# Heads' sums turned in 32x32 squares on VectorE, and row maxima brought to rows by a transpose and two transfers through scratch DRAM

## Chip, cores and metric

The kernel runs on one core of a Trainium2 chip. The metric is the device time of one execution in microseconds; the time before is the median of three runs.

## What is computed

Eight sequences of 512 tokens with 256 features pass through four transformer layers with six attentions in all. Every attention has 16 heads of 16 features:

```python
q, k, v = x @ wq + bq, mem @ wk + bk, mem @ wv + bv      # split into 16 heads of 16
s = einsum('bhqd,bhkd->bhqk', q, k) * scale + bias        # window, causal or full
a = softmax(s)
o = einsum('bhqk,bhkd->bhqd', a, v).reshape(B, L, D)
out = o @ wo + bo                                         # then a residual and a layernorm
```

Attention 0 sees a window of 64 keys, attention 2 is causal, and 1, 3, 4 and 5 are full. After attentions 1, 3 and 4 comes a feed-forward block of 1024 hidden features. Everything is float32.

## The kernel before

A loop is one attention of one sequence. There are 48: the sequences go in pairs (slots), and within a pair the order is attention 0 of both, attention 1 of both and so on. All five engines run through one list of stages, PLAN, each taking its own part of every stage in order and waiting on semaphores for the others. The list for a loop is merged from four streams: 0 is the loop's own steps, 1 is the maxima of its later heads, 2 is the tail of the loop before (output product, feed-forward, layernorm) and the start of the next loop, and 3 is the context work of the next loop. The strings in MERGE say, digit by digit, from which stream the next stage comes; there is one string for each kind of loop.

**Scores and maxima.** The scores that go into the exponential come from bfloat16 parts that lie packed in rows of two tiles (q_packed and k_packed, line 686), with the query's negated row maximum as one more row, MAXROW. So the maximum has to be known, as a row over the queries, before a group's first scores. For that the scores are computed a second time, coarsely, queries on partitions (stage "max", line 655, 128 queries by up to 512 keys), and VectorE reduces them to one bfloat16 column of row_max for each head and block of 128 queries (line 921 where the attention is full, line 924 otherwise). Heads go in groups of four. When a group's 16 columns are there, stage "max_rows" follows: TensorE multiplies them by the identity (line 664, four matmuls of 128 columns into a score pair of PSUM), ScalarE copies the four rows to SBUF (line 817) and issues a transfer into MAXROW of q_packed (line 820). TensorE waits for it at the group's first scores (line 678).

**Steps.** A step is a group of heads and a block of 128 keys, 16 steps a loop. TensorE makes the scores of two heads at a time into one of two score pairs ("st"), ScalarE takes the exponential (line 834) and TensorE adds up the values of the four heads in four strips of 32 partitions of one bank ("pv", line 711); a 17th column of ones in the values gives the sums. After a group's last step ScalarE copies the bank to sums (line 843).

**Heads.** Stage "heads" turns sums, so that queries lie on partitions: four transposes on TensorE into one of the three banks "mx" (line 720), then VectorE's reciprocal of the 17th columns (line 933) and the multiply into tile o (line 935). At the end of the loop, in its tail, stage "turn_heads" turns o back, features on partitions, as the output product needs it: four transposes for each half of the features (line 727) into a score pair, copied to oT by ScalarE (line 847). The product (line 774, stage "rows", or line 748, stage "add") waits for these copies.

The three mx banks also take the maxima, the projections and the output products, and a bank is free again when VectorE (or ScalarE) has read it. Tile oT also holds "pre", the normalised input of attention 4. SyncE's queue carries the weights, the inputs and the bfloat16 parts through DRAM (lines 516 and 544); ScalarE's queue carries the maxima (line 820) alone. GpSimd masks the queries of a head for its maxima (line 1005), among other things.

Of the kernel before, what the change touches and what calls it, by code (L numbers as in the profile page):

```python
# [23 lines left out]
AHEAD = GRP + 2  # L24
RING = 4
# [88 lines left out]
def max_column(h, i):  # L114

    return ((NG - 1 - h // GRP) * TT + i) * GRP + h % GRP


def maxima_stages(b, a, heads):

    for h in heads:
        if h and h + RING - 1 < H:
            yield "mask", b, a, h + RING - 1
        for i in range(TT):
            yield "max", b, a, h, i
        if h % GRP == GRP - 1:
            yield "max_rows", b, a, h // GRP

# [54 lines left out]
def prefetched(b, a):  # L183

    return a == 0 and b >= SLOTS
# [45 lines left out]
def streams(j):  # L231
# [14 lines left out]
    "first": "022001141101110111001111444141110101111000111101101141110410111010111011011001141012222222222202"  # L246
           "422444242444224244424244444220204042200242222402200422240220044000400",
    "01": "011101122111011201111212112301210111301101111011012011110211002121012001100111210110012122222322"
           "22020220200222020220020222022000222202220200222",
    "10": "010013001101113022110120111101021212222020101100110112111010110100011211010110101121101011001021"  # L250
           "131222222222020222002020222020022202000220022220200220202202000",
    "11": "011011022111012110212122220201010221110101121100101111211121220001210111000112222220020112011021"
           "10110210001010012222220222220202022202202022202220220020022222022020002202000",
    "20": "011110101121210121111101211222220022111021011100101110211002222001211101221212220102010101101110"
           "0012011000220021222222222222020222022220002022220222000222220222022200",
    "21": "030011212111013010110011111210111011211011011100101102111221222113111211021101010101210012020022"
           "2222022020222020202202202202202000200222202022020220002",
    "30": "010110221110121102121122222321103011011011100110201101112101100001111100010110101101101011001010"
           "213222222222020222002020222020022202000220022220200220202202000",
    "31": "011011022111012110212122220201010221123310333233111211112111123311132111102222202021123201102200"  # L260
           "022210202001120010110201112100021222223322202202202022002202022202002202000002222200022020220200"
           "0",
    "40": "011011022111012110212122220201010221123310333233111211112111123311132111102222202021123220110220"
           "002220202001120002111001121101002122222332220220220202200220202220200220200000222220002202022020"
           "00",
    "41": "011011020111032231100102111211011121112111121111211311112011021101200110010110100110031000012222"
           "22222002220220202202020222002020200222202022000220200200000000",
    "50": "011011020111032231100102111211011121112111121111211311112011022211012001100101101001100310000122"
           "2222222002220220202202020222002020200222202022000220200200000000",
# [883 lines left out]
```

## Time and profile before

| | |
|---|---|
| median of three runs | 3678.9 us (3677.79 to 3679.34) |
| profiled execution | 3676.84 us |
| its span | 3675.0 us |
| mean granted TensorE clock | 0.996 |
| instructions | 56922 |

The span reaches from the first to the last instruction of the program in the profile; the 1.8 us between it and the execution's time lie around it. The profile counts an engine as busy while one of its instructions runs; matmuls are pipelined and overlap in it.

### The profile page before, as it was taken

The numbers are of one execution on the slowest core, as the hardware profiler recorded it, in microseconds if no ns is written. First come the engines' busy times: TensorE is split into PE (matmuls) and PEld (weight loads), VectorE is DVE, ScalarE is ACT, GpSimd is POOL, SyncE is SP. The second block draws the span as 40 slices with busy tenths as digits, with TensorE's granted clock in tenths as the row PEclk, the third lists the DMA queues.
The fourth block names the chain that finished last, engine by engine and source line by source line (L and its number), as shares of the span: only waits on it lengthen the run. The fifth ranks groups of instructions, "written<-read, shape, count | busy, mean of one in ns | idle before, by whom it ended". The sixth has DMA issues, their size and how long they took to land.

```text
span 3675.0 us, 56922 instructions
## 1 busy us (share of the span) xinstructions
PE 3594.9 (98%) x20572; PEld 1822.7 (50%) x20852; DVE 2355.5 (64%) x6039; ACT 2083.7 (57%) x2663; POOL 1140.6 (31%) x1053
## 2 busy tenths in 40 slices
PE   8999999999999999999999999999999999999998
PEld 5555545443554555544364555554436455455443
DVE  4765776655675586665677558665567855766556
ACT  2555565555555565655656546555575655655555
POOL 4322432222532242222253223222235322322222
PEclk9999999999999999999999999999999999999999
DMA  6312311212321231121232122112133212211111
GB/s 222 104 44 75 104 53 52 84 58 87 106 74 47 75 104 44 52 84 58 87 122 84 47 85 69 47 63 71 63 108 106 85 52 84 71 42 62 61 52 52
DMA packets 260119, 279.28 MB, mean 76 GB/s; under 512 B 25074, under 2 KB 251250, under 8 KB 255858
## 3 DMA queue, kind: packets, MB, share of 16 engines
q1 hardware_dynamic: 258308, 274.84, 22.9%
q8 instruction: 170, 2.79, 0.3%
q14 instruction: 105, 0.86, 0.1%
q10 hardware_dynamic: 1536, 0.79, 0.1%
HBM read 195.05 MB, written 79.69 MB: 75 GB/s over the span
## 4 chain that ended last, share of the span: by engine, by line
PE 92%; DVE 3%; ACT 2%; issue 2%; SPq 1%; DMA 0%; ACTq 0%; POOL 0%; DVEq 0%; POOLq 0%; another core or an unknown queue 0%
PE pv L711 16%; PE st L686 15%; PE mx L655 14%; PE mx L774 10%; PE mx L630 9%; PE st L738 9%; PE st L639 5%; PE mx L748 4%; PE mx L720 2%; PE mx L771 2%; ACT probs L834 2%; PE st L664 1%; PE st L784 1%; DVE mx L924 1%; PE st L727 1%
## 5 line engine op out<-in xcount | busy, mean ns | idle before, releaser
L834 ACT ACTIVATE probs<-st 128x1024 f32<-128x1024 f32 (+1 forms) x1344 | 1261.1, 977 | 643.4 <-PE st L686 401.1
L921 DVE TENSOR_REDUCE row_max<-mx 128x1 bf16<-128x512 f32 x2048 | 1293.9, 687 | 421.9 <-PE mx L655 271.3
L1005 POOL TENSOR_TENSOR qm<-q_high,own_rows 128x512 bf16<-128x512 bf16 x768 | 791.7, 1039 | 1643.6 <-PE mx L655 1033.1
L686 PE MATMUL st<-q_packed,k_packed 97*128 97x512 bf16 (+2 forms) x3072 | 810.5, 344 | 24.7 <-issue 9.2
L655 PE MATMUL mx<-k_high,qm 128*128 128x512 bf16 (+4 forms) x2792 | 797.2, 341 | 14.0 <-DVE row_max L924 2.8
L711 PE MATMUL pv<-probs,va 128*32 128x512 f32 (+2 forms) x6144 | 703.4, 531 | 8.9 <-ACT probs L834 6.9
L655 PEld LDWEIGHTS mx<-k_high,qm 128*128 128x128 bf16 x3072 | 281.9, 97 | 485.3 <-issue 116.2
L686 PEld LDWEIGHTS st<-q_packed,k_packed 97*128 97x128 bf16 (+1 forms) x3072 | 279.6, 98 | 402.9 <-ACT probs L834 122.9
L924 DVE CUSTOM_DVE_ANT_0 mx<-mx,tab 128x192 f32<-128x192 f32 (+4 forms) x1024 | 402.5, 443 | 108.1 <-PE mx L655 103.1
L738 PE MATMUL st<-xT,w1s 128*128 128x512 f32 x768 | 343.3, 593 | 1.9 <-ACT xT L863 1.5
L948 DVE TENSOR_TENSOR y<-mx,row 128x256 f32<-128x256 f32 x224 | 95.0, 424 | 345.1 <-PE mx L774 340.7
L1017 POOL TENSOR_TENSOR rstd<-spread_of,m_half 128x2 f32<-128x2 f32 x144 | 99.3, 690 | 691.8 <-DVE spread_of L967 691.8
L854 ACT ACTIVATE hid<-st,col 128x512 f32<-128x512 f32 x192 | 121.4, 683 | 253.7 <-PE st L738 253.7
L711 PEld LDWEIGHTS pv<-probs,va 128*32 128x32 f32 x6144 | 124.9, 108 | 251.3 <-issue 178.4
L774 PE MATMUL mx<-w2s,hid 128*128 128x256 f32 x1024 | 231.6, 380 | 0.0
L738 PEld LDWEIGHTS st<-xT,w1s 128*128 128x128 f32 x768 | 144.8, 190 | 157.4 <-issue 149.0
L774 PEld LDWEIGHTS mx<-w2s,hid 128*128 128x128 f32 x1024 | 190.0, 191 | 22.7
L630 PE MATMUL mx<-xT,sq 128*128 128x512 f32 x352 | 165.2, 615 | 9.3 <-DMA sq<-squares_dram 8.0
L774 PE MATMUL mx<-sq,oT 128*128 128x256 f32 x640 | 164.7, 380 | 0.0
L863 ACT ACTIVATE xT<-st,col 128x256 f32<-128x256 f32 x192 | 96.7, 561 | 106.1 <-PE st L784 106.1
L817 ACT ACTIVATE max_rows<-st 4x512 bf16<-4x512 f32 x192 | 111.2, 579 | 72.0 <-PE st L664 71.4
L843 ACT ACTIVATE sums<-pv 128x512 f32<-128x512 f32 x192 | 114.8, 598 | 62.4 <-PE pv L711 58.8
(93 smaller groups left out, 3525.3 us busy)
## 6 DMA issues: line engine op xcount, KB each, us to landing
k_packed<-k_parts_dram SPq DMA_DIRECT2D x576, 128.0 KB, 2.7
q_packed<-q_parts_dram SPq DMA_DIRECT2D x576, 128.0 KB, 2.7
q_parts_dram<-q_low SPq DMA_DIRECT2D x96, 256.0 KB, 2.1
k_parts_dram<-k_low SPq DMA_DIRECT2D x96, 256.0 KB, 2.1
q_parts_dram<-q_high SPq DMA_DIRECT2D x48, 256.0 KB, 2.1
k_parts_dram<-k_high SPq DMA_DIRECT2D x48, 256.0 KB, 2.2
w1s<-w_dram SPq DMA_DIRECT2D x12, 1024.0 KB, 5.0
w2s<-w_dram SPq DMA_DIRECT2D x12, 1024.0 KB, 7.2
```

The lines of the kernel that those rows point to most:

```text
L630: mm = pe.matmul(bank, sqw(f"{m}{a}")[:, j, t * P:(t + 1) * P], src[:, j, :], start=(j == 0), stop=(j == KT - 1))
L639: mm = pe.matmul(pair[:, i // 2, i % 2 * D:(i % 2 + 1) * D], source(b, a)[:, j, i * P:(i + 1) * P], sqw(f"v{a}")[:, j, :], start=(j == 0), ...
L655: mm = pe.matmul(bank[:, 0:k1 - k0], qm[:, h % RING, i * P:(i + 1) * P], high["k"][s][:, t, k0:k1], start=True, stop=True)
L686: mm = pe.matmul(flat[:, c:c + w], kk[:, k * P:(k + 1) * P], qq[:, q0:q1], start=True, stop=(k_kind == FULL))
L711: mm = pe.matmul(pv[j * PAIR:(j + 1) * PAIR, q0:q1], va[s][:, k, at:at + PAIR], probs[:, step % 2, c:c + q1 - q0], start=(k == 0 and k_kin ...
L738: mm = pe.matmul(pair[:, e], w1s[:, j, at:at + P], xT[s][:, j, :], start=(j == 0), stop=(j == KT - 1))
L748: mm = pe.matmul(bank, weight[:, j, t * P:(t + 1) * P], src[:, j, :], start=(j == 0), stop=(j == count - 1))
L774: mm = pe.matmul(bank[:, 0:D], src[:, j, i * P:(i + 1) * P], weight[:, j, :], start=False, stop=(j == count - 1))
L834: act.activation(dst[:, :, 0:w], held["scores", b, a, n, e][:, :, 0:w], ACT.Exp, scale=ATT_SCALE[a]) \
L921: ins = dve.tensor_reduce(top, scores, AX_X, ALU.max, negate=True)
L924: ins = dve.tensor_tensor_reduce(scores, scores, hide[:, hide.shape[1] - (k1 - k0):hide.shape[1]], -1.0, 1e30, ALU.add, ALU.min, top)
L1005: pool.tensor_tensor(qm[:, h % RING], high["q"][s][:, h // HT], own_rows[:, h % HT:h % HT + 1].to_broadcast([P, TOK]), ALU.mult) \
```

## The change

Stage "heads" leaves TensorE. VectorE transposes sums in SBUF in squares of 32x32 (tile turned), takes the reciprocal, multiplies into a second tile (normal), and after every second group transposes that tile in squares straight into oT. A strip of 32 partitions holds one head's 17 rows, so a square holds one head and 32 queries; two groups fill the 32 rows of a strip with 16 + 16 features, which puts the heads in another order, place(h). The columns of the value weights, their biases and the rows of the output weights are put in that order on the host. Stage "turn_heads", with its matmuls and its copies on ScalarE, is gone; the output product waits for VectorE. "pre" moves from oT to the first part of the tile hid.

Stage "max_rows" leaves TensorE too. VectorE transposes the group's block of row_max (128 partitions by 32 columns, bfloat16) in squares, ScalarE issues a transfer to scratch DRAM that puts the pieces in order (128 pieces of 64 bytes), and in a new stage "max_back", placed behind the maxima of the next group's first head (for the last group, directly behind max_rows), ScalarE waits for this transfer and issues another, 4 KB, into MAXROW of q_packed. All MERGE strings are new.

```diff
+def place(h):
+    return h // HT * HT + h % GRP * 2 + h // GRP % 2
...
 def max_column(h, i):
-    return ((NG - 1 - h // GRP) * TT + i) * GRP + h % GRP
+    return h // GRP * BLK + h % GRP * TT + i
...
             yield "max_rows", b, a, h // GRP
+        if h % GRP == 0 and h or h == H - 1:
+            yield "max_back", b, a, (h - 1) // GRP
...
     yield "heads", b, a, NG - 1
-    yield "turn_heads", b, a, 0
-    yield "turn_heads", b, a, 1
...
-            return {"ctx": ncT, "pre": oT}.get(tag, xT[b % SLOTS])
+            return {"ctx": ncT, "pre": pre}.get(tag, xT[b % SLOTS])
...
-                elif kind == "max_rows":
-                    a, g = stage[2:]
-                    pe.wait_ge(*mx_drained.past(("max", b, a, g * GRP + GRP - 1, TT - 1)))
-                    pair = held["row", b, a, g] = st_pair()
-                    for i in range(TT):
-                        c = max_column(g * GRP, i)
-                        mm = pe.matmul(pair[:, 0, i * P:(i + 1) * P], row_max[s][:, c:c + P], tb("eye"), start=True, stop=True)
-                    mm.then_inc(*st_filled.mark(("row", b, a, g)))
...
-                elif kind == "heads":
-                    a, g = stage[2:]
-                    pe.wait_ge(*sums_kept.past(("sums", b, a, g)))
-                    bank = held["heads", b, a, g] = mx_bank()
-                    for i in range(TT):
-                        mm = pe.transpose(bank[:, i * P:(i + 1) * P], sums[:, g % 2, i * P:(i + 1) * P], eye[:])
-                    mm.then_inc(*mx_filled.mark(("heads", b, a, g)))
-                elif kind == "turn_heads":
...
                 elif kind == "max_rows":
                     a, g = stage[2:]
-                    act.wait_ge(*st_filled.past(("row", b, a, g)))
-                    act.activation(max_rows[:, g % 2], held["row", b, a, g][0:GRP, 0], ACT.Identity) \
-                        .then_inc(*st_drained.mark(("row", b, a, g)))
-                    act.wait_ge(*st_drained.past(("row", b, a, g)))
-                    act.dma_start(packed["q"][MAXROW:MAXROW + 1, g * GRP:(g + 1) * GRP], max_rows[:, g % 2]) \
+                    act.wait_ge(*row_step.past(("max_rows", b, a, g)))
+                    act.dma_start(r_dram[g].rearrange("(r k) c -> k r c", k=P // BLK), max_rows[:, g]).then_inc(max_row_out[g], 16)
+                elif kind == "max_back":
+                    a, g = stage[2:]
+                    act.wait_ge(max_row_out[g], 16 * (LOOP_NO[b, a] + 1))
+                    act.dma_start(packed["q"][MAXROW:MAXROW + 1, g * GRP:(g + 1) * GRP], r_dram[g, 0:GRP * TT * P // BLK]) \
                         .then_inc(max_row_in[g], 16)
...
-                        act.wait_ge(*mx_filled.past(("heads", pb, pa, (g - 2) % NG)))
+                        act.wait_ge(*row_step.past(("turned", pb, pa, (g - 2) % NG)))
...
+                elif kind == "max_rows":
+                    a, g = stage[2:]
+                    j = LOOP_NO[b, a]
+                    if j:
+                        dve.wait_ge(max_row_out[g], 16 * j)
+                    dve.wait_ge(*mx_drained.past(("max", b, a, g * GRP + GRP - 1, TT - 1)))
+                    dve.transpose(max_rows[:, g], row_max[s][:, g * BLK:(g + 1) * BLK]) \
+                        .then_inc(*row_step.mark(("max_rows", b, a, g)))
                 elif kind == "heads":
                     a, g = stage[2:]
-                    dve.wait_ge(*mx_filled.past(("heads", b, a, g)))
...
+                    t, odd = divmod(g, 2)
+                    old = (b, a, g - 1) if g else (*before(b, a), NG - 1) if LOOP_NO[b, a] else None
+                    blocks = turned[:].rearrange("p (n c) -> p n c", c=BLK)
+                    shares = normal[:].rearrange("p (n c) -> p n c", c=BLK)[:, :, odd * HD:(odd + 1) * HD]
+                    dve.wait_ge(*sums_kept.past(("sums", b, a, g)))
+                    if old:
+                        dve.wait_ge(*row_step.past(("shares", *old)))
+                    chain(dve.transpose(turned[:], sums[:, g % 2]), ("turned", b, a, g))
+                    chain(dve.reciprocal(rec[:], blocks[:, :, HD]), ("rec", b, a, g))
+                    if old and not odd:
+                        dve.wait_ge(*row_step.past(("oT", old[0], old[1], old[2] // 2)))
+                    share = dve.tensor_tensor(shares, blocks[:, :, 0:HD],
+                                              rec[:].unsqueeze(2).to_broadcast([P, TOK // BLK, HD]), ALU.mult)
+                    share.then_inc(*row_step.mark(("shares", b, a, g)))
+                    if odd:
+                        if LOOP_NO[b, a] and not t:
+                            pb, pa = before(b, a)
+                            dve.wait_ge(*mx_filled.past(("add", pb, "a4", KT - 1) if pa == 4 else ("rows", pb, f"a{pa}", TT - 1)))
+                        dve.wait_ge(*row_step.past(("shares", b, a, g)))
+                        dve.transpose(oT[:, t], normal[:]).then_inc(*row_step.mark(("oT", b, a, t)))
...
+    for a in range(6):
+        square[f"v{a}"], square[f"o{a}"] = square[f"v{a}"][:, order], square[f"o{a}"][order]
...
+        args.append(nc.dram_tensor("rows_of_max_dram", (NG, P, BLK), BF16, kind="Internal").ap())
```

## Rows read from the trace of the kernel before

**Rows 1.** The page: span, engines' busy time, the chain's shares by line.
```profile
span 3675.0 us, 56922 instructions
...
PE 3594.9 (98%) x20572; PEld 1822.7 (50%) x20852; DVE 2355.5 (64%) x6039; ACT 2083.7 (57%) x2663; POOL 1140.6 (31%) x1053
...
PE pv L711 16%; PE st L686 15%; PE mx L655 14%; PE mx L774 10%; PE mx L630 9%; PE st L738 9%; PE st L639 5%; PE mx L748 4%; PE mx L720 2%; PE mx L771 2%; ACT probs L834 2%; PE st L664 1%; PE st L784 1%; DVE mx L924 1%; PE st L727 1%
```

**Rows 2.** Timeline of TensorE, two windows: start us, busy us, engine, line, count.
```profile
100.31 0.63 PE L720 MATMUL mx<-eye,sums 128*128 128x128 f32 x4
100.77 0.60 PE L727 MATMUL st<-eye,o 128*128 128x128 f32 x4
101.21 0.30 PE L655 MATMUL mx<-k_high,qm 128*128 128x128 bf16 x2
...
2598.15 0.40 PE L664 MATMUL st<-tab,row_max 128*128 128x128 bf16 x4
2598.39 0.60 PE L655 MATMUL mx<-k_high,qm 128*128 128x512 bf16 x2
2598.82 0.60 PE L686 MATMUL st<-q_packed,k_packed 97*128 97x512 bf16 x2
2599.25 0.38 PE L655 MATMUL mx<-k_high,qm 128*128 128x512 bf16 x1
...
2600.21 1.07 PE L711 MATMUL pv<-probs,va 128*32 128x512 f32 x8
```

**Rows 3.** Groups by line: count | busy us, mean ns | idle us before.
```profile
L720 PE MATMUL mx<-eye,sums 128*128 128x128 f32 x768 | 116.5, 274 | 0.8 <-ACT sums L843 0.7
...
L817 ACT ACTIVATE max_rows<-st 4x512 bf16<-4x512 f32 x192 | 111.2, 579 | 72.0 <-PE st L664 71.4
...
L935 DVE TENSOR_TENSOR o<-mx,rec 128x256 f32<-128x256 f32 x192 | 81.5, 425 | 6.6
...
L664 PE MATMUL st<-tab,row_max 128*128 128x128 bf16 x768 | 75.2, 221 | 2.4 <-DVE row_max L924 2.4
...
L727 PE MATMUL st<-eye,o 128*128 128x128 f32 x384 | 58.4, 279 | 0.6 <-DVE o L935 0.4
L847 ACT ACTIVATE oT<-st 128x512 f32<-128x512 f32 x96 | 56.2, 595 | 7.2 <-PE st L727 7.2
...
L933 DVE RECIPROCAL rec<-mx 128x16 f32<-128x16 f32 x192 | 48.2, 251 | 13.6 <-PE mx L720 13.0
```

**Rows 4.** VectorE by line; for L921 and L973 duration ns min/median/max.
```profile
L962 DVE BATCH_NORM_STATS2 st<-y 128x6 f32<-128x256 f32 x288 | 107.9, 417 | 2.1
...
L967 DVE TENSOR_SCALAR spread_of<-moments 128x2 f32<-128x2 f32 x144 | 24.4, 169 | 5.0
...
L921 DVE TENSOR_REDUCE row_max<-mx x2048: 680/684/697, 132.8 to 3637.6; 128x1 bf16<-128x512 f32 x187
...
L973 DVE TENSOR_SCALAR y<-y,moments,rstd x288: 401/408/1426, 117.5 to 3667.6; 128x256 f32<-128x256 f32 x144
```

**Rows 5.** Windows, one loop each: length; busy us (count) PE, PEld, DVE, ACT, POOL; PEclk.
```profile
1051.70:1117.60 65.90, 64.97 (x358) 28.48 (x366) 52.34 (x99) 43.90 (x53) 23.02 (x21) 1.00 0.24 75
1859.40:1905.20 45.80, 44.60 (x431) 30.14 (x428) 35.50 (x167) 24.02 (x35) 30.23 (x27) 1.00 0.36 114
1616.90:1708.00 91.10, 89.84 (x395) 37.10 (x400) 48.40 (x81) 48.97 (x59) 20.76 (x18) 1.00 0.19 60
```

**Rows 6.** DMA issues: count, KB, us to landing; for L820 the issue's ns.
```profile
k_packed<-k_parts_dram SPq DMA_DIRECT2D x576, 128.0 KB, 2.7
...
q_parts_dram<-q_low SPq DMA_DIRECT2D x96, 256.0 KB, 2.1
...
L820 ACTq DMA_DIRECT2D q_packed<-max_rows x192: 580/581/1174, 27.6 to 3640.5; - x192
```

**Rows 7.** Timeline at the start of a loop, and the window from there on.
```profile
1002.37 0.26 PE L686 MATMUL st<-q_packed,k_packed 106*128 106x192 bf16 x1 [2.45 <-DMA q_packed<-q_parts_dram]
...
1002.40:1005.80 3.40, 3.40 (x28) 3.26 (x29) 1.96 (x10) 1.41 (x2) 3.28 (x4) 0.70 0.31 109
```

More of the change, by code:

```diff
@@ L276 @@
+    "last": "011100111101000021111100101211110112112100100011011101112111010100110110011001100101101001120000"
+           "020102020200000002000000",
 }
@@ L347, in program @@
         va = [sb(f"va{s}", [P, TT, VROW]) for s in range(SLOTS)]
-        row_max = [sb(f"row_max{s}", [P, TT * H + P], BF16) for s in range(SLOTS)]
+        row_max = [sb(f"row_max{s}", [P, NG * BLK], BF16) for s in range(SLOTS)]
         ncT = sb("ncT", [P, KT, TOK])
         oT = sb("oT", [P, KT, TOK])
-        o = sb("o", [P, TT, D])
+        turned = sb("turned", [P, TOK])
+        normal = sb("normal", [P, TOK])
         y = sb("y", [P, TT, D])
@@ L358, in program @@
         qm = sb("qm", [P, RING, TOK], BF16)
-        max_rows = sb("max_rows", [GRP, 2, TOK], BF16)
+        max_rows = sb("max_rows", [P, NG, BLK], BF16)
         probs = sb("probs", [P, 2, GRP * TOK])
@@ L363, in program @@
         x_next = [hid[:, s * KT:(s + 1) * KT] for s in range(SLOTS)]
+        pre = hid[:, 0:KT]
         flat_hid, flat_w1, flat_w2 = (t[:].rearrange("p k n -> p (k n)") for t in (hid, w1s, w2s))
@@ L426, in program @@
         packed_in = [sem(f"packed{half}_in") for half in range(2)]
+        max_row_out = [sem(f"max_row{g}_out") for g in range(NG)]
         max_row_in = [sem(f"max_row{g}_in") for g in range(NG)]
@@ L624, in _ @@
                         pe.wait_ge(sq_in[a], 16)
-                    src = (oT if a == 4 else x_next[s] if prefetched(b, a) else xT[s]) if m == "q" else source(b, a)
+                    src = (pre if a == 4 else x_next[s] if prefetched(b, a) else xT[s]) if m == "q" else source(b, a)
                     pe.wait_ge(*(input_of(b, a) if m == "q" else keys_of(b, a)))
@@ L714, in _ @@
                     mm.then_inc(*step_done.mark(("values", b, a, n)))
-                elif kind == "heads":
-                    a, g = stage[2:]
-                    pe.wait_ge(*sums_kept.past(("sums", b, a, g)))
-                    bank = held["heads", b, a, g] = mx_bank()
-                    for i in range(TT):
-                        mm = pe.transpose(bank[:, i * P:(i + 1) * P], sums[:, g % 2, i * P:(i + 1) * P], eye[:])
-                    mm.then_inc(*mx_filled.mark(("heads", b, a, g)))
-                elif kind == "turn_heads":
-                    a, t = stage[2:]
-                    pe.wait_ge(*mx_drained.past(("heads", b, a, (t + 1) * NG // KT - 1)))
-                    pair = held["oT", b, a, t] = st_pair()
-                    for i in range(TT):
-                        mm = pe.transpose(pair[:, 0, i * P:(i + 1) * P], o[:, i, t * P:(t + 1) * P], eye[:])
-                    mm.then_inc(*st_filled.mark(("oT", b, a, t)))
                 elif kind == "hidden":
@@ L1050 @@
     zeros = np.zeros(D, np.float32)
+    order = np.zeros(D, int)
+    for h in range(H):
+        order[place(h) * HD:(place(h) + 1) * HD] = np.arange(h * HD, (h + 1) * HD)
     kv2 = L2("Wkv")
@@ L1064 @@
     inner = {f"{m}{a}": L1(f"{pre}_{m}_W") for a, pre in ((2, "sa"), (3, "ca")) for m in "qkv"}
+    for a in range(6):
+        square[f"v{a}"], square[f"o{a}"] = square[f"v{a}"][:, order], square[f"o{a}"][order]
+    for a in FOLDED:
+        outer[f"v{a}"] = outer[f"v{a}"][:, order]
     vec = {}
@@ L1076 @@
         vec[f"b{m}4"] = zeros
+    for a in range(6):
+        vec[f"bv{a}"] = vec[f"bv{a}"][order]
     vec["bo4"] = L2("bo")
```

83 lines of the change are left out of this document (35 added, 48 removed).

## Prediction

> **What bounds the kernel now.** I read the page first: TensorE is busy for 3594.9 of 3675.0 us, VectorE for 64%, ScalarE for 57% [rows 1]. A busy matmul record overlaps its neighbour, so the shares by line of the chain that ended last say more; its first ten lines are all TensorE's, and "mx L720" (turning the heads' sums) holds 2% of the span, "st L664" (maxima to rows) 1% and "st L727" (turning the heads) 1%. The timeline then gives what one such group takes from the engine, from its start to the start of the next one [rows 2]: four L720 transposes 0.46 us (100.31 to 100.77), four L727 transposes 0.44 us (to 101.21), four L664 matmuls 0.24 us (2598.15 to 2598.39). Two maxima of a full loop take 0.43 us, two scores 0.43 us, a step's values 1.07 us. So TensorE is a queue with few holes, and what matters is work taken off it and holes put into it.
>
> **The change part by part.** The profiled execution took 3676.8 us (span 3675.0 and 1.8 us around it), 2.1 us under the median of 3678.9; I sum changes and add them to the median.
>
> *A. Matmuls that go.* By count and pitch: four matmuls to a group, 192 groups of L720 x 0.46 = 88 us, 192 of L664 x 0.24 = 46 us, 96 of L727 x 0.44 = 42 us [rows 2, 3]. Together -176 us. The chain's shares of 2, 1 and 1% of 3675 (147 us as rounded) agree in size.
>
> *B. Holes and buffers that go with them.* TensorE idled 0.8 + 2.4 + 0.6 = 3.8 us right before these groups [rows 3]. ScalarE's copies L817 (111.2 us) and L847 (56.2 us) go, so 288 fewer jobs hold one of the two score pairs in PSUM and 192 fewer hold a max bank. ScalarE is 2% of the chain, 74 us, which is the most that this can give. I take -8, nearer to the 3.8 us seen; bounds 0 and -74.
>
> *C. VectorE's new work.* The trace has no square transpose. Nearest are operations from SBUF: 417 ns for 256 elements (L962) and 169 ns for 2 (L967), a slope of 0.98 ns an element, so 0.67 us for 512 elements and 0.2 us for the 32 of a max block; from PSUM, 512 elements take 684 ns (L921) [rows 4]. Bounds for 512: 0.42 us (as for 256) and 2.7 us (four times L921, if a 4-byte element went byte by byte). I take 0.68, since one pass over the elements is what the rows show for every kind of operation. Reciprocal and multiply stay. A loop (there are 48) gets four turns of sums, two of heads and four small ones: 6 x 0.68 + 4 x 0.2 = 4.9 us, in all 235 us, and VectorE goes from 64% to about 72%. In a loop like 1616.9 to 1708.0 it idles for 43 us and this is hidden by TensorE's own work [rows 5]. 24 loops are tight (VectorE at 0.69 or more of the window): 16 like 1051.7 to 1117.6 (52.3 of 65.9 us busy) and 8 like 1859.4 to 1905.2 (35.5 of 45.8). After a saving of 3.5 us the first kind has 57.2 of 62.4 us, the second 40.4 of 42.3. In-order waits don't let an engine reach 95%; at 92% the second kind needs 43.9 us, 1.6 more, x 8 = 13 us, and I give the first 0.75 us each, 12 us. So +25; bounds 0 and all new work of the tight loops, 24 x 4.9 = 118. Behind a turn on VectorE stand the row maxima that free the three max banks: an odd group now holds the engine for 0.68 + 0.25 + 0.42 + 0.68 = 2.0 us, where it was 0.7.
>
> *C2. A port.* One VectorE operation wholly in SBUF (L973) took 1426 ns where 408 is its median [rows 4]; the difference, 1018 ns, is about one GpSimd mask operation (23.02 us for 21 in [rows 5], 1.1 each). A few such hits among 192 multiplies that now read SBUF twice would be some us of VectorE's time, mostly under cover; I add nothing. The Trainium skill (SBUF — State Buffer, "SBUF: two separate sides") has a rule that speaks against the change: a VectorE operation with two SBUF inputs and a GpSimd operation lock a port pair against each other, and the loser waits for the whole instruction. The trace agrees with a lock of that length; by the rule with every multiply hit the sum would be up to 192 x 1.0 us of VectorE time worse, which is what the rival "VectorE bounds" covers.
>
> *D. The rows come later.* Before, one 4 KB transfer from SBUF. Now VectorE turns a block, ScalarE issues a write to scratch DRAM, and at the stage "max_back" waits for it and issues the read. Nearest landings: 2.1 us for a write to scratch DRAM, 2.7 us for a read [rows 6]. Walking the new stage list with the pitches above, 20 of the 192 reads stand less than 2.7 us of TensorE's work ahead of the scores that need them: loops of attention 4 at groups 2 and 3 (0.4 and 1.3 us, four times each), of attention 3 at group 0 (1.5, four times), attention 0 (1.7, three times), the very last group (0.0), and four more. The shortfalls add to 26 us. TensorE waits there with nothing behind it, in order. +26; bounds 0 (TensorE is itself late) and 46 (each wait 1.0 us longer, if the clock falls as it did after the 2.45 us hole at 1002.37: there it was 0.70 on the mean of 3.4 us, a mix of 1.2 and 2.4 GHz, which costs 0.30 x 3.4 = 1.0 us [rows 7]).
>
> *E. ScalarE's waits.* Its issue takes 0.58 us [rows 6]; a copy of 0.58 goes for each issue that comes, and L847 goes besides, so its work falls by 56 us. But it now stands at "max_rows" for VectorE's last max and turn (159 of 192 such stages stand 0.4 us or less of TensorE's work behind the last max), and at "max_back" for the landing: in 32 groups less than 2.1 us of TensorE's work lies between, short by 34 us in sum. Queued behind are the exponentials; TensorE feels it once both score pairs are full. With ScalarE 57% busy I let half of the 34 through, 17, and 8 for the stands at max_rows: +25; bounds 0 and 100.
>
> *F. The sums' path to the output product.* TensorE's and ScalarE's parts are gone, VectorE's chain is 2.0 us. Four times (second half, attention 1) only 0.8 us of TensorE's work lies between: +5; bounds 0 and 15. "pre" moves to another tile and the weights' columns are reordered on the host: 0. The second read-out of oT waits for the previous product, which stands far ahead in all but four loops, and there just ahead: 0.
>
> Sum: -176 - 8 + 25 + 26 + 25 + 5 = -103, so 3678.9 - 103 = 3576 us. A measurement of this kernel tells 0.2% (7.4 us) from no change.
>
> **The rivals.**
> *Nearly all of it hides* (3505 to 3545, -176 - 8 and then 10 to 50 of the costs). For: 24 loops with idle VectorE; the shortfalls of D fall where TensorE may be late anyway. Against: 20 reads with too little ahead. Chance 0.17.
> *VectorE or ScalarE's queue bounds the short loops* (3615 to 3670). C at 80, D at 40, E at 60 give -176 - 8 + 80 + 40 + 60 + 5 = +1, the far end; with half of each excess over the forecast's terms, 52 us, it is 3628. For: 95% in eight loops, locks. Against: TensorE was 99% busy at 79% VectorE. Chance 0.15.
> *Squares are slow, and the kernel slower.* Place: the turns in the 24 tight loops. Price: these have 65.9 - 3.5 - 52.3 = 10.1 us to spare, less 0.8 for the small turns, so 1.55 us for each of six; above it a loop grows by six times the excess. The gain of 103, with the 25 of C, is used up at 1.55 + 128 / (24 x 6) = 2.44 us a turn; the bound of 2.7 us gives 24 x 6 x 1.15 = 166 us in place of the 25, +38 net, 3717 (3690 to 3850, the other loops having too little cover at its upper end). For: no row shows the operation. Against: every VectorE row is one pass. Chance 0.10.
> *The matmuls go but the time does not*: their time turns into waits on the same VectorE work, within 7.4 us of before. It needs A eaten exactly. Chance 0.04.
>
> **How the numbers follow.** The forecast itself, 3545 to 3615, has 0.52; its two neighbours, both faster, 0.17 and 0.15; under 3505 us 0.02; slower 0.10; same 0.04. The range of 8 in 10 is 3512 to 3668: it holds the forecast and nearly all of its two neighbours, and leaves out the slower case. Faster is the sum of the first four, 0.86; same 0.04, slower 0.10.
>
> **What would show it.** L664, L720 and L727 are gone, the span is about 100 us shorter, and TensorE's idle time grows by some 50 to 80 us. A 128x512 transpose takes 0.6 to 0.75 us (over 1.5: the slow rival). VectorE's share is 71 to 74%. In the list of waits, scores wait for a transfer q_packed<-scratch some 20 times, at attention 4 most of all (else D is wrong); ScalarE's exponentials wait, and TensorE for them, more often than before (E). The tight loops shorten by about 2 us and the others by 3 to 3.5 us (C). A kernel that is slower, or 170 us faster, would prove the size of C to E wrong.

## The result and the profile after

The changed kernel took 3581.1 us (median of four runs, 3578.2 to 3585.4), where the kernel before took 3678.4 beside it: ratio 0.9737, 95% interval 0.9720 to 0.9754, 97 us faster. The forecast was 3576 us (3512 to 3668).

The head of the page, and the chain of waits by engine and by line:

```profile
span 3579.2 us, 53643 instructions
...
PE 3472.6 (97%) x18932; PEld 1656.1 (46%) x18932; DVE 2579.5 (72%) x6519; ACT 1933.9 (54%) x2375; POOL 1145.7 (32%) x1053
...
PE 83%; DVE 12%; ACT 1%; issue 1%; DMA 1%; SPq 1%; POOL 1%; ACTq 0%; DVEq 0%; POOLq 0%
PE pv L712 15%; PE st L687 14%; PE mx L664 13%; PE mx L762 10%; PE st L725 9%; PE mx L639 9%; DVE row_max L905 5%; PE mx L736 4%; PE st L648 4%; DVE mx L908 3%; PE mx L759 2%; PE st L772 1%; DVE y L976 1%; DMA rows_of_max_dram<-max_rows 1%; DVE turned L928 1%
```

Against [rows 1]: TensorE's busy time fell by 122.3 us and its idle time rose from 80.1 to 106.6 us, by 26.5 where the prediction had said 50 to 80. (The trace before lacks 280 of TensorE's matmul records, 20572 beside 20852 weight loads, so both of its figures are a little off.) The three groups that were to leave the chain have left it; VectorE now holds 12% of it, mostly with row maxima. The groups on VectorE (count | busy us, mean ns | idle us before):

```profile
L905 DVE TENSOR_REDUCE row_max<-mx 128x1 bf16<-128x512 f32 x2048 | 1283.4, 684 | 230.9 <-PE mx L664 226.6
L928 DVE STREAM_TRANSPOSE turned<-sums 128x512 f32<-128x512 f32 x192 | 134.6, 701 | 5.4 <-ACT sums L832 5.4
L932 DVE TENSOR_TENSOR normal<-turned,rec 128x256 f32<-128x256 f32 x192 | 90.6, 472 | 6.6
L940 DVE STREAM_TRANSPOSE oT<-normal 128x512 f32<-128x512 f32 x96 | 68.3, 711 | 6.6
L929 DVE RECIPROCAL rec<-turned 128x16 f32<-128x16 f32 x192 | 48.7, 254 | 6.6
L917 DVE STREAM_TRANSPOSE max_rows<-row_max 128x32 bf16<-128x32 bf16 x192 | 40.6, 212 | 20.7 <-DVE row_max L905 0.9
```

The turns take 0.70, 0.71 and 0.21 us, 243.5 us in all (forecast 0.68, 0.68, 0.2 and 235). The list of waits (engine, line, waited for: us, times, longest):

```profile
PEld mx L664 <- DVE row_max L905: 193.0, 338, 1.3
PEld st L687 <- ACT probs L823: 148.9, 228, 0.8
PEld mx L664 <- DVE row_max L908: 83.3, 227, 0.9
PE mx L664 <- DVE row_max L905: 18.2, 54, 1.0
PE mx L664 <- DVE row_max L908: 12.9, 38, 0.7
ACT probs L823 <- DMA rows_of_max_dram<-max_rows: 12.0, 2, 9.2
ACT q_low L792 <- DMA rows_of_max_dram<-max_rows: 11.0, 11, 2.2
...
PEld st L687 <- DMA q_packed<-rows_of_max_dram: 1.5, 1, 1.5
...
PE st L687 <- DMA q_packed<-rows_of_max_dram: 0.6, 1, 0.6
```

The maxima's weight loads wait 276 us for VectorE, where it was 153 (103.8 and 49.5). The scores' wait for the maximum's row, of which the forecast had 20, happens once, in the last group of all. ScalarE's queue (duration ns: min/median/max):

```profile
L805 ACTq DMA_DIRECT2D rows_of_max_dram<-max_rows x192: 510/526/1096, 25.6 to 3543.9; - x192
L809 ACTq DMA_DIRECT2D q_packed<-rows_of_max_dram x192: 200/200/252, 33.3 to 3546.5; - x192
```

Three windows of the changed kernel (us, then busy us by engine, clock, DMA share): the first loop kind and the second, both tight before, and a roomy one.

```profile
1028.80:1092.40 63.60, 62.41 (x323) 24.74 (x323) 56.86 (x109) 40.77 (x47) 22.23 (x21) 1.00 0.25 79
1811.30:1854.70 43.40, 41.87 (x392) 26.78 (x390) 36.58 (x167) 20.39 (x29) 28.15 (x26) 1.00 0.39 123
1480.00:1578.80 98.80, 96.42 (x466) 47.69 (x466) 71.32 (x160) 53.87 (x70) 26.14 (x27) 1.00 0.21 69
```

The first two answer to [rows 5]: the loop of 66.0 us is 63.6 with VectorE at 0.89, the one of 45.8 is 43.4 at 0.84. The third is the surprise: it was 99.0 us, ten groups of matmuls are gone from it (3.7 us by pitch: 4 x 0.46, 4 x 0.24, 2 x 0.44), VectorE idles 28% of it, and it is 0.2 us shorter. Cut at each loop's last copy of sums, and leaving out the first loop, the tight loops give 1.8 us each on the mean, the roomy ones 2.4. These means hide a wide spread. Of the tight ones, attention 3 of the first sequence gives 5.3 us (65.6 to 60.3, VectorE 0.78 busy before), which is more than the 3.7 us of matmuls that it lost, and attention 0 of the second sequence gets longer. Of the roomy ones, attention 4 (second sequence) and 5 (first sequence) give 4.4 and others 0.3.

### The profile page after: what moved, and what is told of

The parts are those of the page before. It is cut to its first block, busy times and chain, and to the rows that moved or that the text cites. A ratio compares the mean times of both kernels' runs of the same rounds, so it can differ in the third digit from the quotient of the medians.

```text
span 3579.2 us, 53643 instructions
## 1 busy us (share of the span) xinstructions
PE 3472.6 (97%) x18932; PEld 1656.1 (46%) x18932; DVE 2579.5 (72%) x6519; ACT 1933.9 (54%) x2375; POOL 1145.7 (32%) x1053
## 4 chain that ended last, share of the span: by engine, by line
PE 83%; DVE 12%; ACT 1%; issue 1%; DMA 1%; SPq 1%; POOL 1%; ACTq 0%; DVEq 0%; POOLq 0%
PE pv L712 15%; PE st L687 14%; PE mx L664 13%; PE mx L762 10%; PE st L725 9%; PE mx L639 9%; DVE row_max L905 5%; PE mx L736 4%; PE st L648 4%; DVE mx L908 3%; PE mx L759 2%; PE st L772 1%; DVE y L976 1%; DMA rows_of_max_dram<-max_rows 1%; DVE turned L928 1%
## 5 line engine op out<-in xcount | busy, mean ns | idle before, releaser
L664 PE MATMUL mx<-k_high,qm 128*128 128x512 bf16 (+4 forms) x3072 | 883.2, 345 | 41.8 <-DVE row_max L905 18.2
L664 PEld LDWEIGHTS mx<-k_high,qm 128*128 128x128 bf16 x3072 | 282.2, 97 | 609.2 <-DVE row_max L905 193.0
L687 PEld LDWEIGHTS st<-q_packed,k_packed 97*128 97x128 bf16 (+1 forms) x3072 | 280.3, 98 | 439.7 <-ACT probs L823 148.9
L639 PE MATMUL mx<-xT,sq 128*128 128x512 f32 x352 | 163.7, 611 | 10.5 <-DMA sq<-squares_dram 8.0
L908 DVE DVE_READ_ACCUMULATOR2_ANT row_max<- 128x1 bf16 x1024 | 147.2, 144 | 0.0
```

Source lines behind the costliest of these rows:

```text
L639: mm = pe.matmul(bank, sqw(f"{m}{a}")[:, j, t * P:(t + 1) * P], src[:, j, :], start=(j == 0), stop=(j == KT - 1))
L664: mm = pe.matmul(bank[:, 0:k1 - k0], qm[:, h % RING, i * P:(i + 1) * P], high["k"][s][:, t, k0:k1], start=True, stop=True)
L687: mm = pe.matmul(flat[:, c:c + w], kk[:, k * P:(k + 1) * P], qq[:, q0:q1], start=True, stop=(k_kind == FULL))
L908: ins = dve.tensor_tensor_reduce(scores, scores, hide[:, hide.shape[1] - (k1 - k0):hide.shape[1]], -1.0, 1e30, ALU.add, ALU.min, top)
```

## Experiments

All of them are against a kernel before of 3677 to 3679 us on the same chip. The changed kernel's own run is 3581.1; it was not run again beside them, so a difference to it compares two chips, on which the kernel before agrees within 1 us. The edits shown are the main lines of each, "..." where lines are left out.

### What the matmuls were worth

**doubled**: the kernel before, with each matmul of L664, L720 and L727 issued twice.

```diff
-                    for i in range(TT):
+                    for i in [*range(TT)] * 2:
```

> The kernel before, with every matmul of lines 664, 720 and 727 issued twice into the same place; nothing else. The forecast's term A (176 us for them once, by their pitch on TensorE): 3678 + 176 = 3854 us, 3835 to 3870. Rival: part of these matmuls lies in waits that were there anyway, and what the change gained, 97 us, is all that they cost: 3775 us, 3755 to 3795.

3818.0 us, ratio 1.0379 (1.0361 to 1.0396): +140, where the pitches say 176, and between the two expectations. TensorE's busy time rose by 170 us (to 3765.3) and its idle time fell from 80.1 to 50.6. So part of such a matmul fits where TensorE waited anyway. If removing is worth what adding costs, which this run doesn't show, the change takes away about 0.8 of the pitch.

**turn_twice**: the same test on the changed kernel, with the four transposes of stage "turn" (L772) twice, 56 us by pitch.

```diff
-                    for j in range(KT):
+                    for j in [*range(KT)] * 2:
```

> The changed kernel with the four TensorE transposes of each stage "turn" issued twice, some 56 us of TensorE's work by pitch. Doubling VectorE's turns cost 120 us for 134 us of work. Theory 1 (the changed kernel sits where both engines set the pace by turns): 35 to 55 us slower than the changed kernel, as TensorE's doubled work in the kernel before cost 0.8 of its pitch. Rival (VectorE alone now sets the pace): less than 15 us slower.

3626.3 us (0.9860 of before, 0.9846 to 0.9875): +45, again 0.8. TensorE still sets the pace after the change, at the same price.

### What VectorE's turns cost

**short_turns**: the changed kernel, with the two large turns cut to 32 of 512 columns from the second loop on (it leaves work out: the rest of turned and oT keeps the first loop's values, so its output is not the kernel's).

```diff
+                    w = BLK if LOOP_NO[b, a] else TOK
-                    chain(dve.transpose(turned[:], sums[:, g % 2]), ("turned", b, a, g))
+                    chain(dve.transpose(turned[:, 0:w], sums[:, g % 2, 0:w]), ("turned", b, a, g))
...
-                        dve.transpose(oT[:, t], normal[:]).then_inc(*row_step.mark(("oT", b, a, t)))
+                        dve.transpose(oT[:, t, 0:w], normal[:, 0:w]).then_inc(*row_step.mark(("oT", b, a, t)))
```

> The changed kernel, but from the second loop on the turns of sums and of heads on VectorE cover 32 of the 512 columns (work left out: the rest of both tiles stays as the first loop left it). That takes some 0.5 us off each of 282 turns, 140 us of VectorE's time. Theory 1, the forecast's split (all new VectorE work costs 25 us of the path): 25 x 140/224 = 16 us faster than the changed kernel, 3560 to 3572. Theory 2, from the trace after (the maxima wait for banks that VectorE frees late, and this is most of what was given back, some 70 us): 40 to 60 us faster, 3520 to 3541.

3565.4 us (0.9692, 0.9677 to 0.9706): -16, though VectorE's busy time fell by 113.5 us (2579.5 to 2466.0).

**two_turns**: the changed kernel, with sums turned twice.

```diff
+                    chain(dve.transpose(turned[:], sums[:, g % 2]), ("first", b, a, g))
```

> The changed kernel with the turn of sums on VectorE done twice, one after the other: 192 x 0.70 = 134 us more of VectorE's time. Theory 1: the 24 tight loops are close to full now, so half of their 67 us come out, the other 24 hide theirs: 20 to 40 us slower than the changed kernel, 3601 to 3621. Theory 2: VectorE already sets the pace in the tight loops and bursts stall TensorE elsewhere: 60 to 110 us slower, 3641 to 3691.

3700.7 us (1.0061, 1.0046 to 1.0076): +120, all of the gain, and more than either expectation. Busy time, and the chain by engine:

```profile
PE 3501.4 (95%) x18932; PEld 1656.8 (45%) x18932; DVE 2737.8 (74%) x6711; ACT 1937.1 (52%) x2375; POOL 1144.7 (31%) x1053
...
PE 64%; DVE 29%; issue 3%; ACT 2%; DMA 1%; SPq 1%; POOL 1%; ACTq 0%; DVEq 0%; POOLq 0%
```

And the group of its multiply:

```profile
L933 DVE TENSOR_TENSOR normal<-turned,rec 128x256 f32<-128x256 f32 x192 | 118.0, 615 | 6.8 <-DVE rec L930 0.2
```

VectorE's busy time rose by 158 us, not 135: the multiply behind the turns now takes 615 ns on the mean (below). Going down by 113 us of VectorE's work gave 16, going up by 158 cost 120, so on this engine removing and adding are not worth the same. The changed kernel stands at the bend, and VectorE's share, 72 or 74%, doesn't show where the bend is.

### The way of the rows through scratch DRAM

**one_hop**: the rows go from SBUF to MAXROW directly, in four pieces, with no scratch DRAM and no "max_back".

```diff
-                    act.dma_start(r_dram[g].rearrange("(r k) c -> k r c", k=P // BLK), max_rows[:, g]).then_inc(max_row_out[g], 16)
+                    for k in range(P // BLK):
+                        act.dma_start(packed["q"][MAXROW:MAXROW + 1, g * GRP:(g + 1) * GRP]
+                                      .rearrange("p h (i k c) -> p (h i) k c", k=P // BLK, c=BLK)[:, :, k],
+                                      max_rows[k * BLK:k * BLK + GRP * TT, g]).then_inc(max_row_in[g], 16)
```

> The changed kernel without the scratch DRAM: ScalarE sends the turned maxima straight into the row in four pieces of 16 partitions each; the stage max_back and its wait are gone. ScalarE issues four transfers a group instead of two, 192 x 2 x 0.58 = 223 us more of its time. Theory 1 (terms D and E: late rows and ScalarE's waits cost 51 us): faster by 20 to 40 us, 3541 to 3561, the added issues taking the rest. Theory 2 (late rows cost nothing, ScalarE's waits little): the added issues decide, 0 to 50 us slower, 3581 to 3631.

3738.8 us (1.0164, 1.0149 to 1.0180): +158, where the dearer expectation had +50 at most. The one landing takes 1.7 us (median), but what counts is the queue (the chain by engine; then the issues, ns min/median/max):

```profile
PE 68%; DVE 13%; ACTq 7%; ACT 6%; issue 3%; POOL 1%; SPq 1%; DMA 1%; DVEq 0%; POOLq 0%
```

```profile
L806 ACTq DMA_DIRECT2D q_packed<-max_rows x768: 510/611/1572, 26.1 to 3700.1; - x192
```

768 issues at 0.61 us are about 470 us of ScalarE's sequencer, where the changed kernel has 192 x (0.53 + 0.20) = 140. The exponentials stand behind them: TensorE's scores wait 55.8 us for them and their loads 233.9 (148.9 in the changed kernel). This kernel has a dearer queue besides having one hop, so it doesn't price the scratch hop by itself.

**pool_back**: "max_back", wait and issue, goes to GpSimd's queue.

```diff
-                    act.wait_ge(max_row_out[g], 16 * (LOOP_NO[b, a] + 1))
-                    act.dma_start(packed["q"][MAXROW:MAXROW + 1, g * GRP:(g + 1) * GRP], r_dram[g, 0:GRP * TT * P // BLK]) \
+                    pool.wait_ge(max_row_out[g], 16 * (LOOP_NO[b, a] + 1))
+                    nc.gpsimd.dma_start(packed["q"][MAXROW:MAXROW + 1, g * GRP:(g + 1) * GRP], r_dram[g, 0:GRP * TT * P // BLK]) \
```

> The changed kernel, but GpSimd instead of ScalarE waits for the write to scratch DRAM and issues the read, at the same place in the order. It takes the wait and 0.2 us of issue a group off ScalarE. Theory 1 (term E: ScalarE's waits cost 17 us): 10 to 20 us faster than the changed kernel, 3561 to 3571. Theory 2 (ScalarE has slack, the trace after shows 23 us of such waits in all): within 7 us, 3574 to 3588. Rival: GpSimd's masks come late behind its wait, slower by over 10 us.

3731.9 us (1.0141, 1.0124 to 1.0158): +151. GpSimd, idle two thirds of the time, waits in order:

```profile
POOL q_packed L1009 <- DMA rows_of_max_dram<-max_rows: 812.6, 154, 23.5
...
PEld mx L664 <- POOL qm L1003: 62.5, 46, 4.1
...
PE mx L664 <- POOL qm L1003: 40.5, 29, 3.6
```

Queued behind its wait are the masked queries, and TensorE waits for those: 62.5 us by the loads, where it was 14.4 in the changed kernel, and 40.5 by the matmuls, where it was 0.7. That is not all of the 151. VectorE's busy time is 68.5 us longer too (2648.0; the multiply takes 657 ns on the mean), TensorE's own waits for row maxima are 76.4 us (31.1), and its mean clock is 0.981 (0.993). How the loss splits among these was not tested. A wait costs what stands behind it.

**late_back**: the changed kernel with "max_back" moved later in the list where less than 2.6 us of TensorE's work lay between it and the write, if 3.3 us stayed ahead of the scores.

```diff
+        while done < 12 and ahead - WORK.get(stages[at][0], 0) >= 15:
+            done, ahead = done + WORK.get(stages[at][0], 0), ahead - WORK.get(stages[at][0], 0)
+            at += 1
+        stages.insert(at, back)
```

> The changed kernel, with the stage that waits for the write and issues the read moved later wherever less than 2.6 us of TensorE's work lies between it and the write, as long as 3.3 us are left ahead of the scores. Theory 1 (ScalarE's waits for the landing, 24 us by the list of waits, reach TensorE by a third or less): 3 to 10 us faster than the changed kernel. Rival (they are hidden by ScalarE's idle time): within 3 us. Rival (reads then come late for scores, as the forecast's step D had it): slower by 10 us or more, with scores waiting for q_packed<-rows_of_max_dram more than once.

3577.9 us (0.9729, 0.9712 to 0.9745): 3 us less, not to be told from none. ScalarE's waits for the write don't get fewer (30.5 us in sum, 23.6 in the changed kernel) and only stand elsewhere:

```profile
ACT probs L844 <- DMA rows_of_max_dram<-max_rows: 18.0, 5, 7.5
...
ACT q_high L808 <- DMA rows_of_max_dram<-max_rows: 12.5, 1, 12.5
```

One of 12.5 us is in the first loop, whose DMA share is 0.68 (in the changed kernel). So moving these waits gains nothing that can be measured.

### Instructions and order, apart

The change has new instructions and a new order (the MERGE strings). The next five kernels part them. "Old rows" are TensorE's matmul and ScalarE's copy; "old heads" are L720 and L727 on TensorE. In the new order the old instructions had no stages of their own, so I had to place them: rows at "max_back", turn_heads three and five stages behind the last "heads".

**rows_back**: new order and heads, old rows.

```diff
+                elif kind == "max_back":
+                        mm = pe.matmul(pair[:, 0, i * P:(i + 1) * P], row_max[s][:, c:c + P], tb("eye"), start=True, stop=True)
...
+                    act.activation(max_rows[:, g % 2], held["row", b, a, g][0:GRP, 0], ACT.Identity) \
```

> The changed kernel with the maxima's rows made as before (four matmuls, ScalarE's copy, one transfer from SBUF), all at the place of the stage max_back in the new order; heads stay on VectorE. TensorE gets 44 us more by pitch, 35 us by the rate of the doubled matmuls (140 for 176). Theory X, both parts gain by their matmuls' share (97 x 44/169 = 25 us): 3606 us, 3598 to 3615. Theory Y, the two transfers and ScalarE's waits (what short turns did not give back, some 27 us) eat the gain of this part: 3575 to 3592 us.

3678.5 us (0.9995, 0.9986 to 1.0005): +97, where the expectations had 34 at most. TensorE's busy time is only 28 us longer (3500.7); the other 71 us are idle time (177.6), spread over many waits: 14.2 us of the row matmuls for the exponentials that hold the score pairs, 10.5 of the scores for the transfer, and smaller ones.

**heads_back**: new order and rows, old heads.

```diff
+        if stage[0] == "heads" and stage[3] == NG - 1:
+            due = [(3, ("turn_heads", *stage[1:3], 0)), (5, ("turn_heads", *stage[1:3], 1))]
...
+                        mm = pe.transpose(bank[:, i * P:(i + 1) * P], sums[:, g % 2, i * P:(i + 1) * P], eye[:])
```

> The changed kernel with the heads' sums turned on TensorE as before, and the turn of heads after the last group three and five stages later, or just ahead of the product; the maxima's rows stay on VectorE and scratch DRAM. Theory X: 72 us slower than the changed kernel, 3653 us, 3640 to 3665. Theory Y (the heads' part brought the whole gain of 97): 3670 to 3685. Should VectorE's turns be worth little, as short turns says (16 us for 140), TensorE's 125 us by pitch x 0.8 = 100 us less that 24 us: 3657 us.

3800.4 us (1.0332, 1.0316 to 1.0347): +219, where the expectations ended at 3685 us. TensorE's busy time is 121 us longer, its idle time 98. Part of that idle time comes from where I placed turn_heads, since the output product waits for its copies (0.7 us in the kernel before):

```profile
PE mx L787 <- ACT oT L864: 18.1, 25, 1.1
```

**both_back**: both edits, so that only the order is new.

> The changed kernel with both parts undone, so the old instructions in the new order of stages. Theory 1: the order is worth little by itself, 3668 to 3690 us, so the gain is that of the two parts. Rival: the new order alone brings part of the gain, 3630 to 3665. Other rival: it is made for the new instructions, and old ones in it stall, over 3700.

3890.8 us (1.0577, 1.0561 to 1.0593): 212 us slower than before. The waits for the copies of oT (18.1 us) and for the rows' transfer (10.5) are here too, so the 212 are not the order's alone.

**new_in_old_order**: the other corner. The old strings, with "max_back" by the change's rule, but for the last group up to four stages behind max_rows; both turns into oT at the last group, where the old order has room for them.

```diff
+            n = at["max", b, a, (g + 1) * GRP, TT - 1] if g + 1 < NG else \
+                min(at["max_rows", b, a, g] + 4, at["scores", b, a, g * TT, 0] - 1)
+            behind.setdefault(n, []).append(("max_back", b, a, g))
...
-                    if odd:
+                    if g == NG - 1:
```

> The new instructions in the order of the kernel before. Its opposite, the old instructions in the new order, took 3890.8 us, 212 more than before. Theory 1 (each order fits its own instructions: the new one leaves VectorE its time where it has turns to make): the old order costs the new instructions 60 us or more, 3640 or longer, with TensorE's waits on VectorE's row maxima longer than 193.0 + 83.3 us. Theory 2 (the order only names the stages differently; the gain is that of the instructions): within 15 us of the changed kernel's 3581. Theory 3 (the old order suits everything that keeps VectorE late): between 3595 and 3640, so the gain is part instructions, part order.

3866.7 us (1.0516, 1.0500 to 1.0531): 189 us slower than before with the same number and kinds of instructions that are 97 us faster in the new order. The turns into oT stand elsewhere than in the changed kernel, though, and that counts below. Its waits:

```profile
PEld mx L678 <- DVE row_max L919: 270.1, 375, 3.3
...
PE mx L678 <- DVE row_max L919: 116.3, 118, 2.9
...
PE mx L678 <- DVE row_max L922: 72.1, 76, 3.3
```

TensorE's own waits for maxima are 188.4 us, where the changed kernel has 31.1. How one comes about, first on VectorE, then on TensorE (start us, busy us, group; idle before in brackets):

```profile
1607.46 0.68 DVE L919 TENSOR_REDUCE row_max<-mx 128x1 bf16<-128x512 f32 x1
1608.06 0.70 DVE L942 STREAM_TRANSPOSE turned<-sums 128x512 f32<-128x512 f32 x1
1608.80 0.25 DVE L943 RECIPROCAL rec<-turned 128x16 f32<-128x16 f32 x1
1609.08 0.42 DVE L946 TENSOR_TENSOR normal<-turned,rec 128x256 f32<-128x256 f32 x1
1609.61 1.30 DVE L957 STREAM_TRANSPOSE oT<-normal 128x512 f32<-128x512 f32 x2
1610.84 3.05 DVE L919 TENSOR_REDUCE row_max<-mx 128x1 bf16<-128x512 f32 x5
```

```profile
1608.35 0.38 PE L678 MATMUL mx<-k_high,qm 128*128 128x512 bf16 x1
1611.55 1.21 PE L678 MATMUL mx<-k_high,qm 128*128 128x512 bf16 x2 [2.83 <-DVE row_max L919]
```

From 1608.06 on VectorE turns for 2.8 us while TensorE is due to make maxima. The three mx banks are full, so TensorE stands for 2.83 us, and it stands in order: nothing behind the maximum starts either. Behind it the clock falls too: its mean is 0.969 in this kernel and 0.993 in the changed one, and with the same 18932 instructions TensorE is busy 3571.7 instead of 3472.6 us. Against the changed kernel, the profiled span is 286 us longer, 99 of it busy time and 187 idle time. Summing TensorE's idle time in the 5 us from the start of each of the 192 turns of sums gives 207.8 us here and 32.8 in the changed kernel. By groups of a loop it is 26.5, 29.4, 31.6 and 120.4 us here and 3.6, 2.2, 21.5 and 5.6 there. So more than half stands behind the last group, as in the burst shown, where two turns into oT follow each other because I placed them so; the old strings with one turn a group were not built. The rest, 87.5 against 27.3 us, has no such burst and points at the order. In the window of this loop VectorE is busy for 66%, so it had the time; it was asked at the wrong moment.

**rows_only**: the kernel before and its order, with only the rows new.

> The kernel before with only the maxima's rows made in the new way (VectorE's small transpose, write to and read from scratch DRAM, each stage where the old order puts it); the heads stay on TensorE. It takes away 192 groups of L664, 46 us by pitch and 37 at the 0.8 that doubling showed, and 111 us of ScalarE's copies, and adds 192 x 0.21 = 41 us to VectorE. Theory 1 (the transfers' waits are covered): 20 to 40 us faster than before, 3638 to 3658. Rival (ScalarE's stands at the write and at the read cost as much as the copies did): within 10 us of before. Rival (the old order has too little room for the landings): slower than before by over 15 us, with scores or exponentials waiting for the scratch transfers by over 60 us.

3693.1 us (1.0045, 1.0030 to 1.0060): 16 us slower than before; my range had been 20 to 40 faster. Of the waits:

```profile
ACT q_low L820 <- DMA rows_of_max_dram<-max_rows: 50.4, 17, 3.3
...
ACT L871 <- DMA rows_of_max_dram<-max_rows: 27.9, 8, 3.8
...
ACT sums L860 <- DMA rows_of_max_dram<-max_rows: 14.3, 3, 11.3
ACT q_high L815 <- DMA rows_of_max_dram<-max_rows: 12.0, 1, 12.0
...
PEld st L701 <- DMA q_packed<-rows_of_max_dram: 6.4, 4, 2.8
PE st L701 <- DMA q_packed<-rows_of_max_dram: 5.4, 5, 1.9
```

ScalarE waits 109 us for the writes (the four rows shown and 4.0 more), against 23.6 in the changed kernel: in the old order "max_back" comes too soon behind the write. By loops, most are 0.6 to 1.1 us shorter; the first is 12 longer, the others of attention 0 together 13, and eight of attentions 3 and 4 together 16.

| rows / heads | old order | new order |
|---|---|---|
| old / old | 3678 (before) | 3891 |
| new / old | 3693 | 3800 |
| old / new | not built | 3678 |
| new / new | 3867 | 3581 (the change) |

(Old rows with new heads in the old order would need a second oT: there the heads of group 1 stand up to 58 stages ahead of the product that still reads the first.) The old instructions lose 212 us by the new order and the new ones gain 286, both with the placement of the stages that I chose for them. The rows alone, in the old order, are worth nothing (16 us slower); the heads alone were not built there, but added to the rows they make the old order 174 us slower. Undoing one part in the new order costs 97 or 219, more than the whole change gave, so such a number is not that part's own worth.

## Why the prediction was right, and where it was not

- **The total** held: -97 for -103. If removing the matmuls gave what doubling them cost, two errors of 36 and 30 us cancelled in it (A and the rest, below), and that was luck.
- **A (the matmuls, -176)** was over-priced, as far as doubling tells. The doubling measured 140. The step that failed was "by count and pitch": a pitch is what a group occupies once it is reached, not what the end moves by; the engine had waits that the group could fill. The 147 us of the chain's shares, which I read as agreement in size, lies near 140 by rounding: unrounded the three shares are 74.9, 50.5 and 36.7 us, 162 in all.
- **B (-8)** was not tested apart. ScalarE's copies went, its busy share fell from 57 to 54%.
- **C (VectorE, +25).** The turn was sized right (0.70 for 0.68), so the rival "squares are slow" fell at once. The cost is of the right size: taking away 113.5 of the 243.5 us was worth 16 us. The tight loops shortened by 1.8 us, forecast 2, but that is a mean of -4.7 to +5.3, so its fit is luck. The roomy ones gave 2.4 and not 3 to 3.5, as unevenly. The split into tight and roomy loops by VectorE's share, and the limit of 92% on an engine that waits in order, had no row behind them: in [rows 5] TensorE, which waits in order too, is busy for 98.6% of a loop, and the two kinds of tight loops ended with VectorE at 0.89 and 0.84. The runs fit another reading better: what counts is what VectorE does when TensorE wants a bank. two_turns shows how close the rival "VectorE bounds" was: 135 us more of such work costs 120.
- **C2 (the port, nothing added)** was small here (9 us of VectorE's time) but real: see below.
- **D (late rows, +26)** was wrong. The walk counted TensorE's work by pitch and took it that TensorE arrives on time; one of the 20 waits was seen, in the place with 0.0 us of room, and the reads land in time elsewhere.
- **E (ScalarE's waits, +25)** was too high. The read's issue takes 0.20 us and not 0.58, and ScalarE waits 23.6 us for writes where I let 34 in and passed on half. At max_rows it waits 34.9 us for VectorE's small turn, of which 8 were passed on. Moving the waits for the writes (late_back) changed nothing that can be measured; what the others cost was not tested.
- **F (+5)**: the product waits 4.7 us for oT in all, 3.0 of that at the end of the kernel; fits.
- **Together**, B to F were forecast at +73 and came to 140 - 97 = 43, a remainder that hangs on the 140. Of these, short_turns accounts for 16, and the loops of attention 0 (second sequence) and the first loop, which became 7.9 and 3.4 us longer in sum, for 11. There (the third such loop) TensorE stands for 3.7 us for q_packed<-q_parts_dram (2.0 before), and the clock falls behind it:

```profile
1855.00:1858.70 3.70, 0.03 (x1) 0.00 (x0) 0.60 (x4) 0.00 (x0) 0.20 (x1) 0.91 0.61 180
1858.70:1862.40 3.70, 3.68 (x21) 3.35 (x22) 1.15 (x7) 1.38 (x2) 1.04 (x1) 0.50 0.64 192
1862.40:1869.20 6.80, 6.80 (x23) 3.77 (x22) 4.08 (x10) 1.61 (x3) 0.00 (x0) 0.82 0.44 137
```

(window, busy us of PE, PEld, DVE, ACT and POOL, granted clock, DMA share.) After a hole of 3.7 us TensorE runs 3.7 us at 0.50, the 1.2 GHz level. Why these parts come later in the new order, I did not test. The last 16 us are unassigned.

What the forecast left out is the order. It priced the new list as it stood, which was enough for the total, but called the gain that of the instructions. The runs show that these instructions are 189 us slower than before in the old list, with the turns into oT placed as said.

## What to carry to other kernels

Work moved to an engine with idle time needs its place in the order as much as its time: ask which buffers fill while the in-order engine does it, and merge the stages anew before judging the move, since one part tried alone in the old order can look useless. Doubling what is to be removed gives a price before it is removed (here 0.8 of the pitch, twice), as far as the engine bounds the kernel on both sides of the change, and doubling what is added shows how far the bend is. A wait is priced by what is queued behind it, not by how idle its engine is.

## Unexpected of the hardware

- **VectorE's multiply, once all its operands lie in SBUF, is at times held until a GpSimd operation ends.** Of the changed kernel and of new_in_old_order:

```profile
L932 DVE TENSOR_TENSOR normal<-turned,rec x192: 424/425/1789, 64.5 to 3560.0; 128x256 f32<-128x256 f32 x192
```

```profile
L946 DVE TENSOR_TENSOR normal<-turned,rec x192: 424/425/1762, 62.3 to 3845.3; 128x256 f32<-128x256 f32 x192
```

Its median is that of the multiply from PSUM (425), its mean 472 and 564 ns, and 615 in two_turns: 9, 27 and 37 us of VectorE's time, by when it happens to fall beside GpSimd's operations, with GpSimd's own work the same. In two_turns the growth from 90.6 to 118.0 us is a sixth of what VectorE's busy time gained. The longest one of the changed kernel, first on VectorE, then on GpSimd:

```profile
917.41 1.79 DVE L932 TENSOR_TENSOR normal<-turned,rec 128x256 f32<-128x256 f32 x1
```

```profile
916.79 2.13 POOL L1014 TENSOR_TENSOR q_low<-q_rest,q_low 128x1024 bf16<-128x1024 f32 x1 [4.07 <-ACT q_low L792]
```

GpSimd's operation ran already when the multiply started, and the multiply ended 0.28 us after it. That is so for all 14 multiplies of the changed kernel that take more than 0.55 us. The other way round, a mask that starts 0.01 us after a multiply (at 308.4 us) takes 1.31 us, where the median is 1.04. The Trainium skill (SBUF — State Buffer, "SBUF: two separate sides") calls the shared port pair "an **exclusive lock**, not a bandwidth split"; the 0.28 us behind GpSimd's end, 14 times of 14, agree with that.
- **An issue on ScalarE's queue is not one price.** 4 KB from DRAM into one partition took 0.20 us; 8 KB out of 128 partitions of SBUF 0.53; a piece of 1 KB out of 16 partitions 0.61.
- **A square transpose of float32 is one pass**: 512 elements 701 ns, and 32 bfloat16 elements 212 ns, a slope of (701 - 212) / 480 = 1.02 ns an element. The Trainium skill (Vector Engine (DVE) Microarchitecture Reference, "3.8 The reshape front-end and per-opcode configuration") has it pipelined at an element a cycle per lane; the length of both rows agrees with one pass, also for 4-byte elements.
